# Moving a softmax sum one step later, a residual sum to GpSimd, and weight products out of the preparation, in a four-layer graph network kernel

## The chip, the core and the metric

The kernel runs on one core of one Trainium2 chip. A core has TensorE (PE in the profile; its weight loads are listed as PEld), VectorE (DVE), ScalarE (ACT), GpSimd (POOL) and SyncE (SP, here used only to issue DMA transfers), and each works through its own queue in order. The metric is the time of one execution on the device in microseconds; lower is better.

## The reference, cut to what matters

A graph has 50,000 nodes with 256 features in float32 and 25,000 edges, sorted by destination. Four layers follow each other, each with a residual and a layer norm. Layer 2 is the one with the most edits:

```python
x = _layernorm(x + L0(x, Wq, Wk, Wv, src, dst))            # attention, sum over edges, 8 heads of 32
x = _layernorm(x + L1(x, edge_index, W1, b1, W2, b2, ...)) # neighbour sum, two products, norm
x = _layernorm(x + L2(x, edge_index, W, att_src, att_dst, bias, ln_w, ln_b))
x = _layernorm(x + L3(x, edge_index, edge_attr, Wq, bq, ..., Ws, bs))

def L2(x, edge_index, W, att_src, att_dst, bias, ln_w, ln_b):   # the edges and one loop per node
    h = (x @ W).reshape(n, H, C)
    e = einsum(h, att_src)[src] + einsum(h, att_dst)[dst]
    e = where(e > 0, e, 0.2 * e)
    ex = exp(e - segment_max(e, dst)[dst])
    alpha = ex / segment_sum(ex, dst)[dst]
    out = segment_sum(h[src] * alpha, dst) + bias
    y = out + x
    return (y - mean(y)) / sqrt(var(y) + EPS) * ln_w + ln_b
```

Layer 2 therefore has two norms: its own ("inner", over the 256 features of `out + x`) with a weight and a bias, and then the common one ("outer") over `x + L2(x)`.

## The kernel before, in words

The nodes are worked on in 196 units of 256 nodes (two tiles of 128, one node to a partition). The program is a sequence of stages that follow each other: the preparation (lists of edges by node tile, weights, constants), layer 0 over edge chunks and nodes, the nodes of layer 1 together with layer 2's projection (`nodes1`, which writes the projected rows `hh_d`), the nodes of layer 2 (`nodes2`), the edges of layer 3 and the nodes of layer 3 (`nodes3`).

Within a stage nothing is scheduled by a compiler: every engine has a function `body(s, at)` that is unrolled for steps s = 0, 1, ..., and in step s a piece with lag L handles unit s - L:

```python
def run_units(total, depth, body):
    for s in range(total + depth):
        body(s, lambda lag: s - lag if 0 <= s - lag < total else None)
```

So the lag and the place in `body` set the order of an engine's queue. Engines wait for each other by semaphores, and for free places in rings of buffers. The softmax of layers 2 and 3 is made once for a group of `GU` = 8 units, with the scores laid out as one row for each node tile and head, by scans along the row: `tops` is the group whose maxima are made in this step, `shares` the one whose sums and shares (the alpha) are made.

`nodes2` in step s, before the change, engine by engine:

- SyncE loads the unit's one-hot matrix `hot` (source edge to node; a ring of `HOT` = 18), at lag 12 the projected rows `hin` and edge attributes `attr`, at lag 14 the residual input `xin` (a ring of `XR` = 9), and stores `e_row`.
- GpSimd gathers the sources' rows of the step's unit by two indirect DMAs into a ring of `NR` = 16 places, and at lag 16 adds `xin` to the node's own message `own`:

```python
if u < NR: gp.wait_ge(zeroed, u + 1)
else:      gp.wait_ge(weighed, u - NR + 1)
```

- TensorE transposes `hot` (lag 2) and `attr` (lag 14), makes the edge product with `w3_e` for layer 3 and the destination's scores, and at lag 17 aggregates: `agg = hot x weighted + bias + own`. It also turns the shares of a group (`share_ps`) at lag 14.
- VectorE, in the order of its queue: reciprocals and shifts of both norms (`norm_invert`, `norm_shift`, inner lag 19, outer lag 22), the group's scans at lag 12 (maxima) and 13 (sums), spread in between, `own` (lag 15), inner statistics on `agg` (18), outer statistics `norm_measure` (21), `scaled` = agg x ln_w (20), merging of the inner statistics (18), `weighted` = gathered rows x share (15), merging of the outer statistics (21), and last the residual sum `outer_rows` = agg + xin (L1422, lag 20).
- ScalarE copies what TensorE made (`turned`, `att_edge`, `e_row`), applies both norms (inner lag 19, outer lag 22), takes the square roots (18 and 21) and the exponential (12), and stores.

VectorE announces `weighed` after `weighted`, `inner["filled"]` comes from TensorE after `agg`, `outer["filled"]` after the residual sum, and `scaled_done` after `scaled`. Groups of layer 3 (`nodes3`) go the same way with fewer pieces.

The shift of a norm is one VectorE instruction for both tiles of a unit, `shift = moments x -1 x rstd` (L478), with two tensor operands. The preparation's VectorE work runs: masks on the edges' ends (`below_lo` and others), the first edge column of each node tile (`first_cast`, from a transfer `first_col` by SyncE), then the weight products: `w2_h` times the attention vectors, `gin`, `w3_s` plus identity, and the biases split into three bf16 parts (`b3`, `bias3`). The list of edges by tile is loaded back as `pairs` by SyncE at the head of layer 0.

## Time and profile before

| | before |
|---|---|
| median of 3 runs | 5031.09 us (5024.81 to 5033.5) |
| the profiled execution | 4998.33 us, of which the span is 4996.6 us |
| mean granted TensorE clock | 0.938 |
| busy share | PE 91%, PEld 70%, DVE 80%, ACT 56%, POOL 50% |
| DMA | 970.10 MB, mean 194 GB/s |
| stages (about, us from the start) | preparation to 55.5, layer 0 to 1093, nodes1 to 2486, nodes2 to 3600, edges of layer 3 to 4257, nodes3 to the end |

The span is the profiler's time from the first to the last instruction of the one profiled execution; the time of that execution is a little longer, and the runs beside it are without the profiler. A busy share is over the whole span, so it mixes stages with different limits; the granted clock is the share of full speed (2.4 GHz) that TensorE was given in a stretch, 0.5 being 1.2 GHz.

### The profile page before, as it was taken

To read this page: it belongs to the slowest core of one execution; us is meant where nothing else is said; L and a number is where in the kernel's file an instruction comes from. 1 tells how busy PE (TensorE), PEld (TensorE's weight loads), DVE (VectorE), ACT (ScalarE), POOL (GpSimd) and SP (SyncE) were. 2 spreads that over 40 slices of the span, in tenths; PEclk is the share of its full clock that TensorE was granted. 3 is DMA by queue.
4 is the path that set the end of the run, shared out by engine and by line. 5 is a ranking of instruction groups with operands and counts; after the bars stand their busy time and mean duration, and the time that the engine had idled before them with its cause. 6 is when DMAs were issued, how large, how long until landed. Compare 5 with 4: busy or idle time off the path is not lost. (4 is left out here: it accounts for less than half of the span.)

```text
span 4996.6 us, 90737 instructions
## 1 busy us (share of the span) xinstructions
PE 4563.9 (91%) x21673; PEld 3506.0 (70%) x21722; DVE 3986.5 (80%) x13147; ACT 2805.1 (56%) x6326; POOL 2476.3 (50%) x2462
## 2 busy tenths in 40 slices
PE   4999998779999999999888888888799999699998
PEld 3666664448888888888767777777566666577777
DVE  4777778979999999999859999999855555567666
ACT  1787886545555555555547777777611111366565
POOL 3555551237777777777466666666365554000000
PEclk8999996569999999999979999999899999899999
DMA  6777778954444444444468888787555554677775
GB/s 138 210 225 222 223 223 257 298 187 135 150 152 153 149 148 152 153 153 148 143 184 252 244 244 244 243 243 243 183 172 163 163 164 146 193 228 228 223 228 160
DMA packets 911233, 970.10 MB, mean 194 GB/s; under 512 B 104899, under 2 KB 867258, under 8 KB 910892
## 3 DMA queue, kind: packets, MB, share of 16 engines
q1 hardware_dynamic: 500692, 471.58, 32.9%
q10 hardware_dynamic: 327416, 315.35, 18.6%
q0 software_dynamic: 82784, 179.41, 12.3%
q8 instruction: 119, 1.95, 0.2%
q14 instruction: 222, 1.82, 0.1%
HBM read 654.56 MB, written 363.57 MB: 204 GB/s over the span
## 5 line engine op out<-in xcount | busy, mean ns | idle before, releaser
L1186 POOL DMA_INDIRECT nodes_near_rows<-hh_d,source_row x392 | 394.9, 1007 | 401.3 <-DVE nodes_weighted L1403 292.6
L586 POOL DMA_INDIRECT layer_xg<-in_x,edge_rows x392 | 386.7, 987 | 358.5 <-PE layer_t_ps L627 241.5
L884 POOL DMA_INDIRECT nodes_near_rows<-x_d,nodes_cur x392 | 419.0, 1069 | 238.2 <-POOL nodes_cur L879 170.8
L1542 POOL DMA_INDIRECT edges_xg<-x_d,edge_rows x392 | 372.9, 951 | 264.3 <-PE edges_x_ps L1568 172.6
L485 ACT ACTIVATE nodes_x<-nodes_outer_rows,nodes_outer_shift,nodes_outer_rstd 128x256 f32<-128x256 f32 x784 | 428.0, 597 | 61.1 <-issue 51.4
L1597 ACT ACTIVATE edges_xT<-edges_x_ps 128x512 f32<-128x512 f32 x196 | 117.1, 597 | 524.7 <-PE edges_x_ps L1568 524.7
L1806 PE MATMUL nodes_agg<-w_s,nodes_xT 128*128 128x256 f32 x1568 | 405.5, 381 | 0.0
L1004 PE MATMUL nodes_h_ps<-w_h,nodes_x2T 128*128 128x272 f32 x1568 | 392.2, 393 | 8.1 <-ACT nodes_x2T L1081 8.1
L660 PE MATMUL layer_agg<-layer_msg,layer_hot 128*128 128x264 f32 x784 | 314.2, 540 | 73.5 <-issue 65.7
L642 PE MATMUL layer_kv_ps<-w_kv,layer_xT 128*128 128x512 f32 x784 | 372.3, 597 | 1.0 <-DVE layer_made L751 1.0
L994 PE MATMUL nodes_out_ps<-w_b,nodes_hid 128*128 128x256 f32 x1568 | 371.2, 380 | 1.4 <-DVE nodes_inner_rows L925 0.8
L1014 PE MATMUL nodes_hid_ps<-nodes_zT,w_a 128*128 128x256 f32 x1568 | 370.5, 379 | 0.7 <-ACT nodes_zT L1088 0.7
L1633 DVE TENSOR_TENSOR edges_kv<-edges_kv_ps,edges_e_row 128x512 f32<-128x512 f32 x196 | 135.5, 692 | 295.2 <-PE edges_kv_ps L1584 295.2
L1584 PE MATMUL edges_kv_ps<-w_kv,edges_xT 128*128 128x512 f32 x784 | 368.4, 592 | 2.6
L660 PEld LDWEIGHTS layer_agg<-layer_msg,layer_hot 128*128 128x128 f32 x784 | 191.6, 260 | 219.3 <-issue 191.8
L1004 PEld LDWEIGHTS nodes_h_ps<-w_h,nodes_x2T 128*128 128x128 f32 x1568 | 297.3, 190 | 65.8 <-ACT nodes_x2T L1081 10.0
L899 POOL TENSOR_TENSOR nodes_x2b<-nodes_x,row_L_gnn_ln_b 128x512 f32<-128x512 f32 x196 | 265.8, 1356 | 142.0 <-DMA x_d<-nodes_x2b 131.4
L485 ACT ACTIVATE layer_y<-layer_ln_rows,layer_ln_shift,layer_ln_rstd 128x256 f32<-128x256 f32 x392 | 213.8, 592 | 217.0 <-DVE layer_ln_shift L478 217.0
L1014 PEld LDWEIGHTS nodes_hid_ps<-nodes_zT,w_a 128*128 128x128 f32 x1568 | 297.8, 190 | 46.5 <-ACT nodes_zT L1088 1.1
L1806 PEld LDWEIGHTS nodes_agg<-w_s,nodes_xT 128*128 128x128 f32 x1568 | 284.6, 191 | 31.0
L994 PEld LDWEIGHTS nodes_out_ps<-w_b,nodes_hid 128*128 128x128 f32 x1568 | 282.6, 190 | 32.4 <-issue 1.0
L941 DVE SCALAR_TENSOR_TENSOR nodes_scaled<-nodes_inner_rows,nodes_inner_moments,row_L_gnn_gamma 128x256 f32<-128x256 f32 x392 | 300.8, 806 | 0.0
(223 smaller groups left out, 12341.3 us busy)
## 6 DMA issues: line engine op xcount, KB each, us to landing
nodes_xin<-x_d SPq DMA_DIRECT2D x588, 256.0 KB, 3.8
layer_msg<-msg_d SPq DMA_DIRECT2D x392, 132.0 KB
hh_d<-nodes_hh ACTq DMA_DIRECT2D x196, 264.0 KB, 4.1
nodes_msg<-msg_d SPq DMA_DIRECT2D x392, 132.0 KB, 3.1
x_d<-layer_y ACTq DMA_DIRECT2D x196, 256.0 KB, 3.8
x_d<-nodes_x2b ACTq DMA_DIRECT2D x196, 256.0 KB, 3.5
nodes_hin<-hh_d SPq DMA_DIRECT2D x196, 256.0 KB, 3.9
x_d<-nodes_x ACTq DMA_DIRECT2D x196, 256.0 KB
```

What stands on the lines that cost most here:

```text
L485: last = nc.scalar.activation(to[:, h, :], t["rows"][:, ring(u, 4), h, :], ACT.Identity, bias=t["shift"][:, ring(u, 4), h:h + 1], scale=t[ ...
L586: gp.indirect_dma_start(out=xg[:, c % 8, k, :], out_offset=None, in_=x, in_offset=bass.IndirectOffsetOnAxis(ap=edge_rows[:, c, k:k + 1], a ...
L642: last = nc.tensor.matmul(kv_ps[b][:, :], xT[:, b, 0, i, :], w0_kv[:, i, :], start=i == 0, stop=i == KC - 1)
L660: last = nc.tensor.matmul(agg[u % 2][:, h, 0:D + H], hot[:, u % 4, h, :], msg[:, r, h, :], start=True, stop=True)
L884: gp.indirect_dma_start(out=near_rows[:, r, h, :], out_offset=None, in_=x1_d, in_offset=bass.IndirectOffsetOnAxis(ap=cur[:, r, h:h + 1], a ...
L994: last = nc.tensor.matmul(out_ps[ring(u, 2)][:, h * D:(h + 1) * D], hid[:, ring(u, 2), k, h * P:(h + 1) * P], w1_b[:, k, :], start=k == 0, ...
L1004: last = nc.tensor.matmul(h_ps[:, h, 0:D + 2 * H], x2T[:, ring(u, 2), k, h, :], w2_h[:, k, :], start=k == 0, stop=k == KC - 1)
L1014: last = nc.tensor.matmul(hid_ps[:, m * 2 * P:(m + 1) * 2 * P], w1_a[:, k, m * P:(m + 1) * P], zT[:, ring(u, 2), k, :, :].rearrange("p h n ...
L1186: gp.indirect_dma_start(out=near_rows[:, u % NR, h, :], out_offset=None, in_=hh_d, in_offset=bass.IndirectOffsetOnAxis(ap=source_row[:, 2 ...
L1542: gp.indirect_dma_start(out=xg[:, c % 8, k, :], out_offset=None, in_=x3_d, in_offset=bass.IndirectOffsetOnAxis(ap=edge_rows[:, c, k:k + 1] ...
L1584: last = nc.tensor.matmul(kv_ps[r][:, :], xT[:, b, 0, j, :], w3_kv[:, j, :], start=False, stop=j == KC - 1)
L1806: nc.tensor.matmul(to, xT[:, u % 2, k, h, :], w3_s[:, k, :], start=k == 0, stop=False)
```

## The change

There are three parts. **(1) Preparation and layer 0.** The weight products and split biases leave the preparation: they become twelve pieces that VectorE runs in twelve steps of layer 0 from step `U0` + 56, and their small loads are issued by ScalarE at the head of layer 0. Of the edges' ends only the destinations are cast before the first masks, the sources after them. The masks of layer 0 are made at `U0` + 24 instead of `U0` + 6, and the `pairs` are loaded during units 8 to 15 instead of ahead of unit 0. **(2) `nodes2`.** The sums of a group are made in step 14 instead of 13, and all that follows moves one step later: share transposes, `own` and `weighted` (15 to 16), GpSimd's own addition (16 to 17), aggregation (17 to 18), inner statistics (18 to 19), `scaled` (20 to 21), outer statistics (21 to 22), the outer shift and its application (22 to 23). `HOT` goes from 18 to 19; `NR` stays at 16. `scaled` writes to the outer norm's rows in SBUF instead of to `agg` in PSUM, and GpSimd adds `xin` to them at lag 21, as the last piece of its step; VectorE's residual sum (L1422) is gone. TensorE waits for `scaled_done` instead of `outer["filled"]` before it reuses an `agg`. The shifts are made by `norm_shift_halves`, one `tensor_scalar` for each tile. **(3) `nodes3`.** The sums and all that follows (share transpose, `weighted`, transposes of `xin`, aggregation, norm, store) are one step later; nothing else changes there.

The diff, cut to what the rest refers to (lags that only grow by one are left out):

```diff
-    LOADS = 11 + len(rows) + 2 + BV + 2
+    LOADS = 11 + len(rows) + 2
...
-                for k in (1, 0):
-                    ve.wait_ge(edges_in[k], 48)
-                    nc.vector.tensor_copy(ends_f[:, k, :, :], ends_c[:, k, :, :]).then_inc(cast, 1)
-                for k in (1, 0):
-                    last = nc.vector.tensor_copy(pairs[:, :, :, k], ends_c[:, k, :, :])
-                last.then_inc(paired, 1)
+                ve.wait_ge(edges_in[1], 48)
+                nc.vector.tensor_copy(ends_f[:, 1, :, :], ends_c[:, 1, :, :]).then_inc(cast, 1)
+                nc.vector.tensor_copy(pairs[:, :, :, 1], ends_c[:, 1, :, :])
...
+                    if mask is below_lo:
+                        ve.wait_ge(edges_in[0], 48)
+                        nc.vector.tensor_copy(ends_f[:, 0, :, :], ends_c[:, 0, :, :]).then_inc(cast, 1)
+                        nc.vector.tensor_copy(pairs[:, :, :, 0], ends_c[:, 0, :, :]).then_inc(paired, 1)
...
-                link(nc.vector.tensor_tensor(b3[:, 0:D], b3[:, 0:D], rows["L2_gnn_ln_b"][0:3, :], ALU.subtract))
...
-                link(nc.vector.tensor_copy(bias3[0:3, :], b3_sum[:, :]))
...
+    def norm_shift_halves(ve, t, u):
+        ve.wait_ge(t["inverted"], num(u) + 1)
+        for h in range(2):
+            last = nc.vector.tensor_scalar(t["shift"][:, ring(u, 4), h:h + 1], t["moments"][:, ring(u, 4), h, 0:1],
+                                           t["rstd"][:, ring(u, 4), h:h + 1], -1.0, ALU.mult, ALU.mult)
+        last.then_inc(t["shifted"], 1)
...
-        MASKS = U0 + 6
+        MASKS, WEIGHTS = U0 + 24, U0 + 56
...
-                sp.wait_ge(lists_out, 16)
-                for h in range(H):
-                    sp.dma_start(pairs[h * 2 * GU:(h + 1) * 2 * GU, 0:WHOLE, :],
-                                 windows[0:WHOLE * 2 * GU, :].rearrange("(g w) x -> w g x", w=2 * GU)).then_inc(pairs_in, 16)
-                    sp.dma_start(pairs[h * REST:(h + 1) * REST, WHOLE, :], windows[WHOLE * 2 * GU:TILES, :]).then_inc(pairs_in, 16)
                 for u in range(UNITS):
+                    if 8 <= u < 8 + H:
+                        h = u - 8
+                        sp.wait_ge(lists_out, 16)
+                        sp.dma_start(pairs[h * 2 * GU:(h + 1) * 2 * GU, 0:WHOLE, :],
+                                     windows[0:WHOLE * 2 * GU, :].rearrange("(g w) x -> w g x", w=2 * GU)).then_inc(pairs_in, 16)
+                        sp.dma_start(pairs[h * REST:(h + 1) * REST, WHOLE, :], windows[WHOLE * 2 * GU:TILES, :]).then_inc(pairs_in, 16)
...
+                for k, name in enumerate(("L2_gnn_att_src", "L2_gnn_att_dst")):
+                    act.dma_start(att[:, k, :], row(a[name], D)).then_inc(more_in, 16)
+                for k, name in enumerate(split_biases):
+                    act.dma_start(b3[:, k * D:(k + 1) * D], row(a[name], D, 3)).then_inc(more_in, 16)
...
+                def weights(piece):
+                    if piece == 0:
+                        ve.wait_ge(more_in, (2 + BV) * 16)
+                        link(nc.vector.tensor_tensor(b3[:, 0:D], b3[:, 0:D], rows["L2_gnn_ln_b"][0:3, :], ALU.subtract))
+                        nc.vector.tensor_scalar(gin[:, :], gin[:, :], 1.0, None, ALU.add)
+                    elif piece <= 2 * KC:
+                        k, j = (piece - 1) // 2, (piece - 1) % 2
+                        link(nc.vector.tensor_tensor(wprod[:, :], w2_h[:, k, 0:D], att[:, j, :], ALU.mult))
+                        link(nc.vector.tensor_reduce(watt[:, k, j * H:(j + 1) * H],
+                                                     wprod[:, :].rearrange("p (h c) -> p h c", h=H), axis=AX.X, op=ALU.add))
+                    elif piece == 2 * KC + 1:
+                        nc.vector.tensor_copy(w2_h[:, :, D:D + 2 * H], watt[:, :, :])
+                    elif piece <= 3 * KC + 1:
+                        k = piece - 2 * KC - 2
+                        nc.vector.tensor_tensor(w3_s[:, k, k * P:(k + 1) * P], w3_s[:, k, k * P:(k + 1) * P], ident[:, :], ALU.add)
+                    elif piece <= 3 * KC + 4:
+                        k = piece - 3 * KC - 2
+                        link(nc.vector.tensor_copy(b3_part[:, :], b3[:, :]))
+                        link(nc.vector.tensor_tensor(b3[:, :], b3[:, :], b3_part[:, :], ALU.subtract))
+                        if k == 0:
+                            link(nc.vector.tensor_scalar(b3_sum[:, :], b3_part[:, :], ident[0:3, 0:1], None, ALU.mult))
+                        else:
+                            link(nc.vector.scalar_tensor_tensor(b3_sum[:, :], b3_part[:, :], ident[0:3, k:k + 1], b3_sum[:, :],
+                                                                ALU.mult, ALU.add))
+                    else:
+                        link(nc.vector.tensor_copy(bias3[0:3, :], b3_sum[:, :]))
...
+                    if WEIGHTS <= s < WEIGHTS + 12:
+                        weights(s - WEIGHTS)
...
-        NR, HR, XR, WR, HOT, LATER = 16, 5, 9, 4, 18, 12
+        NR, HR, XR, WR, HOT, LATER = 16, 5, 9, 4, 19, 12
...
-                    u = at(16)
+                    u = at(17)
                     if u is not None:
                         gp.wait_ge(own_done, u + 1)
                         gp.wait_ge(x_in[u % XR], u // XR * 16 + 16)
                         gp.tensor_tensor(own[:, u % WR, :, :], own[:, u % WR, :, :], xin[:, u % XR, :, :], ALU.add).then_inc(based, 1)
-                run_units(UNITS, 16, body)
+                    u = at(21)
+                    if u is not None:
+                        scaled = outer["rows"][:, u % 4, :, :]
+                        gp.wait_ge(scaled_done, u + 1)
+                        gp.tensor_tensor(scaled, scaled, xin[:, u % XR, :, :], ALU.add).then_inc(outer["filled"], 1)
+                run_units(UNITS, 21, body)
...
-                            pe.wait_ge(outer["filled"], u - 3)
+                            pe.wait_ge(scaled_done, u - 3)
...
-                    tops, shares = (g // GU if g is not None and g % GU == 0 else None for g in (at(12), at(13)))
-                    u = at(19)
+                    tops, shares = (g // GU if g is not None and g % GU == 0 else None for g in (at(12), at(14)))
...
-                        norm_shift(ve, inner, (None, 8, u))
-                    u = at(22)
-                    if u is not None:
-                        norm_shift(ve, outer, (None, 8, u))
+                    u = at(20)
+                    if u is not None:
+                        norm_shift_halves(ve, inner, (None, 8, u))
+                    u = at(23)
+                    if u is not None:
+                        norm_shift_halves(ve, outer, (None, 8, u))
...
-                        nc.vector.tensor_tensor(in_halves(agg[u % 4]), in_halves(agg[u % 4]), both(rows["L2_gnn_ln_w"]), ALU.mult)\
+                        if u >= 4:
+                            ve.wait_ge(outer["normed"], u - 3)
+                        nc.vector.tensor_tensor(outer["rows"][:, u % 4, :, :], in_halves(agg[u % 4]), both(rows["L2_gnn_ln_w"]), ALU.mult)\
...
                             .then_inc(scaled_done, 1)
...
-                    u = at(15)
+                    u = at(16)
                     if u is not None:
                         of_tiles = head_columns(share_ps, of_group(u // GU))
                         ve.wait_ge(share_turned, u // GU + 1)
...
-                    u = at(20)
-                    if u is not None:
-                        ve.wait_ge(scaled_done, u + 1)
-                        ve.wait_ge(x_in[u % XR], u // XR * 16 + 16)
-                        if u >= 4:
-                            ve.wait_ge(outer["normed"], u - 3)
-                        nc.vector.tensor_tensor(outer["rows"][:, u % 4, :, :], in_halves(agg[u % 4]), xin[:, u % XR, :, :], ALU.add)\
-                            .then_inc(outer["filled"], 1)
```

## Rows read from the trace of the kernel before

**Rows 1.** Windows: stretch, length, busy PE, PEld, DVE, ACT, POOL (xinstructions), clock, DMA share, GB/s:

```profile
55.50:125.00 69.50, 46.49 (x155) 29.54 (x156) 22.29 (x57) 13.81 (x36) 42.67 (x45) 0.77 0.86 182
125.00:790.00 665.00, 662.82 (x2583) 409.34 (x2581) 478.74 (x1885) 526.41 (x1005) 347.90 (x352) 1.00 0.72 217
2623.50:3488.40 864.90, 763.73 (x4362) 641.35 (x4360) 793.41 (x2800) 622.76 (x1561) 526.35 (x480) 0.93 0.80 245
```

**Rows 2.** Timeline, GpSimd, 3019 to 3028: start, duration, instruction, idle before it:

```profile
3019.22 1.02 POOL L1186 DMA_INDIRECT nodes_near_rows<-hh_d,source_row  x1 [4.13 <-DVE nodes_weighted L1403]
...
3021.57 1.27 POOL L1193 TENSOR_TENSOR nodes_own<-nodes_own,nodes_xin 128x512 f32<-128x512 f32 x1
3023.55 1.02 POOL L1186 DMA_INDIRECT nodes_near_rows<-hh_d,source_row  x1 [0.72 <-issue]
```

**Rows 3.** Timeline, VectorE and TensorE, one ordinary step:

```profile
3020.71 0.73 DVE L458 BATCH_NORM_STATS2 nodes_outer_parts<-nodes_outer_rows 128x6 f32<-128x256 f32 x2
...
3022.11 0.65 DVE L1403 TENSOR_TENSOR nodes_weighted<-nodes_near_rows,nodes_share_ps 128x512 f32<-128x512 f32 x1
...
3022.84 0.66 DVE L1422 TENSOR_TENSOR nodes_outer_rows<-nodes_agg,nodes_xin 128x512 f32<-128x512 f32 x1
...
3023.26 0.44 PE L1250 MATMUL nodes_work_ps<-ident,nodes_hot 128*128 128x128 f32 x2
...
3027.65 0.20 PEld L1250 LDWEIGHTS nodes_work_ps<-ident,nodes_hot 128*128 128x128 f32 x2 [0.21 <-ACT nodes_e_row L1489]
```

**Rows 4.** Waits, 2500 to 3600: who waits, for whom: total us, times, longest:

```profile
POOL nodes_near_rows L1186 <- DVE nodes_weighted L1403: 292.6, 145, 4.1
DVE nodes_outer_rstd L474 <- ACT nodes_outer_dev L469: 53.1, 54, 2.3
DVE nodes_score_ps L1133 <- ACT nodes_score_ps L1499: 30.5, 25, 3.2
```

**Rows 5.** Window in a group's softmax:

```profile
3005.00:3011.00 6.00, 5.09 (x15) 3.64 (x16) 6.00 (x26) 3.73 (x10) 3.29 (x3) 0.50 0.40 127
```

**Rows 6.** Timeline, VectorE and GpSimd, the step with the sums:

```profile
3002.69 0.72 DVE L458 BATCH_NORM_STATS2 nodes_outer_parts<-nodes_outer_rows 128x6 f32<-128x256 f32 x2
...
3005.09 0.65 DVE L1403 TENSOR_TENSOR nodes_weighted<-nodes_near_rows,nodes_share_ps 128x512 f32<-128x512 f32 x1
...
3006.53 1.02 POOL L1186 DMA_INDIRECT nodes_near_rows<-hh_d,source_row  x1 [3.54 <-DVE nodes_weighted L1403]
```

**Rows 7.** Groups: count | busy us, mean ns of one | idle before:

```profile
L899 POOL TENSOR_TENSOR nodes_x2b<-nodes_x,row_L_gnn_ln_b 128x512 f32<-128x512 f32 x196 | 265.8, 1356 | 142.0 <-DMA x_d<-nodes_x2b 131.4
...
L478 DVE SCALAR_TENSOR_TENSOR nodes_inner_shift<-nodes_inner_moments,nodes_inner_rstd 128x2 f32<-128x2 f32 x195 | 49.8, 255 | 0.1
...
L478 DVE SCALAR_TENSOR_TENSOR nodes_outer_shift<-nodes_outer_moments,nodes_outer_rstd 128x2 f32<-128x2 f32 x192 | 29.9, 156 | 0.0
```

**Rows 8.** Timeline, a held shift and GpSimd's addition:

```profile
3013.48 1.63 DVE L478 SCALAR_TENSOR_TENSOR nodes_inner_shift<-nodes_inner_moments,nodes_inner_rstd 128x2 f32<-128x2 f32 x1
...
3013.81 1.27 POOL L1193 TENSOR_TENSOR nodes_own<-nodes_own,nodes_xin 128x512 f32<-128x512 f32 x1
```

**Rows 9.** Timeline of the preparation and the head of layer 0:

```profile
15.75 0.29 DVE L344 CAST prepare_ends_f<-prepare_ends_c 98x256 f32<-98x256 int32 x1 [7.22 <-DMA prepare_ends_c<-in_src]
...
39.93 0.40 DVE L375 TENSOR_TENSOR prepare_b<-prepare_b,row_L_gnn_ln_b 3x256 f32<-3x256 f32 x1
...
41.58 0.32 SPq L304 DMA_DIRECT2D first_col<-first_edges  x1
...
53.85 0.68 DVE L393 CAST bias<-prepare_b_sum 3x1024 bf16<-3x1024 f32 x1
...
121.36 2.10 PE L660 MATMUL layer_agg<-layer_msg,layer_hot 128*128 128x264 f32 x4 [7.88 <-DMA layer_msg<-msg_d]
```

**Rows 10.** DMA issues: name, engine, count, KB each:

```profile
layer_pairs<-windows SPq DMA_DIRECT2D x8, 384.0 KB
```

**Rows 11.** Timeline, TensorE, layer 3's nodes:

```profile
4514.49 0.30 PE L1785 MATMUL nodes_share_ps<-ident,nodes_share 128*128 128x128 f32 x1 [1.87 <-DVE nodes_weighted L1718]
```

More of the change, by code:

```diff
@@ L218, in marked, with row @@
         return mark, settle
+    def row(ap, n, parts=P):
+        return bass.AP(ap.tensor, ap.offset, [[0, parts], [1, n]])
     def prepare(sb, ps, sem, sems, block):
@@ L253, in prepare @@
         first_cast, first_out, first_in, d, pl = sem("first_cast"), sem("first_out"), sem("first_in"), sem("d"), sem("pl")
-        def row(ap, n, parts=P):
-            return bass.AP(ap.tensor, ap.offset, [[0, parts], [1, n]])
         with block() as blk:
@@ L272, in _ @@
                     load(t[:, :], row(a[name], D))
-                for k, name in enumerate(("L2_gnn_att_src", "L2_gnn_att_dst")):
-                    load(att[:, k, :], row(a[name], D))
-                for k, name in enumerate(split_biases):
-                    load(b3[:, k * D:(k + 1) * D], row(a[name], D, 3))
                 load(gin[:, :], row(a["L1_gnn_eps"], 1))
@@ L1700, in body @@
                     group = group_at(at)
-                    u = at(20)
+                    u = at(21)
                     if u is not None:
                         norm_invert(ve, ln, (None, 8, u))
-                    u = at(15)
+                    u = at(16)
                     if u is not None:
@@ L1724, in body @@
                         mark(top_run(g, n, run[0:n, :], score_ps[0:n, 0:P]))
-                    g = group(12)
+                    g = group(13)
                     if g is not None:
@@ L1729, in body @@
                         mark(sum_run(g, n, run[0:n, :], grown[0:n, :]))
-                    g = group(13)
+                    g = group(14)
                     if g is not None:
@@ L1734, in body @@
                         mark(nc.vector.reciprocal(total[0:n, :], total[0:n, :]))
-                    g = group(14)
+                    g = group(15)
                     if g is not None:
@@ L1757, in body @@
                         nc.vector.tensor_tensor(less[0:n, :], score_ps[0:n, 0:P], top[0:n, :], ALU.subtract).then_inc(less_ready, 1)
-                    g = group(12)
+                    g = group(13)
                     if g is not None:
@@ L1778, in body @@
                         nc.tensor.transpose(score_ps[0:n, 0:P], score[:, 0:n], ident[:, :]).then_inc(score_turned, 1)
-                    g = group(15)
+                    g = group(16)
                     if g is not None:
```

104 lines of the change are left out of this document (44 added, 60 removed).

## The prediction

> **What bounds the kernel now.** I read the stage windows first, then the waits of layer 2's nodes, then its timeline engine by engine, then the two ends of the change (the preparation and the layer 3 nodes). The stages run one after another, so each has its own limit. The long stages that the change touches are layer 0 (TensorE without a gap from 125 us to 790 us), layer 2's nodes and layer 3's nodes. In layer 2's nodes a unit takes 5.41 us: in the steady window of 864.9 us GpSimd has 480 instructions, three to a unit, so 160 units [rows 1]. An ordinary step takes less: GpSimd starts its first gather at 3019.22 and again at 3023.55, 4.33 us later [rows 2]. In such a step three engines are nearly tied. VectorE has no idle time. TensorE goes from transposes to transposes in 4.39 us (3023.26 to 3027.65), and its last wait there is for ScalarE's `e_row` [rows 3]. GpSimd spends 0.7 us before its first gather, 2.35 with the two gathers and 1.28 in the own-message addition, which is all of 4.33 [rows 2]. The missing 1.08 us per unit is lost once per group of eight, around the softmax: the scan waits for ScalarE's exponential (30.5 us in all), VectorE for the outer root (53.1 us) [rows 4], and after TensorE's idle time there its granted clock is 0.50, the 1.2 GHz level, from 3005 to 3011 us [rows 5]. The row that decides this case is another: GpSimd waits 145 times, 292.6 us, for VectorE's `weighted` before it may gather [rows 4]. Its ring of sources has NR = 16 places, `weighted` of unit v is made in step v + 15, and so the gather of step s waits for step s - 1 of VectorE. When the product ends late (3005.09 + 0.65), the gather starts 0.79 us after that end, at 3006.53 [rows 6].
>
> **The change in layer 2's nodes.** It moves `weighted` to step v + 16 and leaves NR at 16. The gather of GpSimd's step s now waits for unit s - 16, which VectorE makes in its own step s, late in it. Behind the gathers, in GpSimd's one queue, stand the own-message addition (unit s - 17) and, new, the residual sum of unit s - 21. VectorE's step s + 1 opens its outer statistics with exactly that sum (`norm_measure(outer)` at lag 22), and makes `weighted` behind them. This closes a ring through two engines, once per step. Each piece has a row:
> - end of `weighted` to the start of the first gather: 0.79 [rows 6];
> - first gather to the start of the own addition: 3021.57 - 3019.22 = 2.35 [rows 2];
> - own addition: 1.28 (1.27 in the row shown) [rows 2]; the residual sum is the same operation on the same shape in SBUF, so 1.28 again. No row shows it in that place; the lower bound is VectorE's 0.66 for the sum that it replaces, the upper one 1.36 (GpSimd's layer 1 sum with a broadcast row) [rows 3, 7];
> - semaphore to VectorE: about 0.05; then start of the outer statistics to the end of `weighted`: 3022.11 + 0.65 - 3020.71 = 2.05 [rows 3].
>
> The sum is 0.79 + 2.35 + 1.28 + 1.28 + 0.05 + 2.05 = 7.80 us a step against 5.41 a unit. Only VectorE work between the outer statistics and `weighted` adds to it. In the step with the sums that is 3005.74 - 3002.69 - 2.05 = 1.0 us [rows 6]; in the step with the maxima I take 0.5 (the less and the top operation, two instructions of the smaller kind). So 1.5 per group. What VectorE saves (0.66 less the price of two more shift instructions at 0.08 spacing each), what it no longer waits for at the scan, and the shifts that are no longer long all lie in the 5.7 us in which it waits for GpSimd, and are worth nothing.
>
> The ring holds from step 21, when the first residual sum is due, to step 195, the last gather: 175 steps with 22 groups. 175 x (7.80 - 5.41) + 22 x 1.5 = 418 + 33 = 451 us. Before step 21 and in the drain I take -5 in all: there GpSimd has no gather in front of the sum, and VectorE has one operation less.
>
> TensorE is then idle for some 3 us in each step, more than the idle time that already costs its clock in every group, so part of its steps will run at 1.2 GHz. Of an ordinary step's 4.39 us about 0.5 is ScalarE's two copies at the end; at half the clock the step is 2 x 3.9 + 0.5 = 8.3 [rows 3, 5]. It may start its aggregation when the own sum is there, 4.4 us after `weighted`, and VectorE needs its result some 12 us after that, so it just fits; in the step with the shares and in that with the scores it is up to 2.5 us late. 0 to 55 us over 22 groups; I take 15, since the clock rises again while it is busy.
>
> A rule of the Trainium skill bears on the sum: GPSIMD Engine Reference, section "Elementwise — side-by-side cycle accounting", has a two-input GpSimd operation at about 2.6 cycles an element, which for 512 elements at 1.2 GHz is an estimate of 1.1 us, and the same page advises against elementwise work there. By that the ring would be 0.2 us shorter and the whole 31 us less; the trace has 1.28, so the row is taken.
>
> **The shift per tile.** `nodes_inner_shift` takes 0.16 us as a rule, but 1.63 us at 3013.48, when GpSimd's own addition (3013.81 + 1.27 = 3015.08) ends just before it does [rows 8]. The groups agree over the stage: 49.8 us for the inner shift, 29.9 for the outer, as many instructions [rows 7]. The new form has one tensor operand instead of two and should not be held. Worth 20 us at most, were VectorE the bound; here nothing. The Trainium skill, SBUF — State Buffer, section "SBUF: two separate sides", says that a VectorE operation with two SBUF inputs and a GpSimd operation that reads SBUF exclude each other; the 1.63 agrees.
>
> **The preparation.** VectorE's weight products run from 39.93 to 54.53 us and end the stage [rows 9]. What is left after `first_cast` is SyncE's round trip: the column of first edges is issued at 41.58 and lands some microseconds later; I take 44.5, so 10 us go. The masks also no longer wait for the sources at 15.75 [rows 9]: the destination's chain starts 6.9 us sooner, of which I take 6. Together -16 (bounds -10 and -18). Layer 0 then opens without the 3 MB of pairs (8 x 384 KB) [rows 10] in front of its x and message loads; TensorE waited 7.88 us for the first message [rows 9], and its clock is 0.77 there [rows 1]. I take -12 (0 to -20). The pairs now travel in units 8 to 15 under a DMA share of 0.72 [rows 1], at no cost as long as TensorE has its chunks; if that cover goes, 3 MB at 217 GB/s are 14 us. The 14.6 us of weight products lie in twelve steps of layer 0 where VectorE is busy 478.74 of 665 us; free time in 12 steps of 7 us is 24 us, but pieces of 3 us are not smooth: +3 (0 to 14.6). ScalarE issues six small loads before its table load, while the first gather is under way: +2 (0 to 6). Together -23.
>
> **Layer 3's nodes.** TensorE loses 1.87 us a group at the share transpose, waiting for `weighted` [rows 11]. Sum, reciprocal, share and transpose all move by one step together, so the same product is late in the same way: VectorE passes three short steps instead of two after the table load and has one scan more in them. I cost it at nothing (within 0.6 us a group, 15 us either way) plus 2 us for one more unit of filling.
>
> **Sum.** 451 - 5 + 15 - 23 + 2 = 440. The profiled execution took 4998.33 us (span 4996.6); it lies 33 us under the median of the runs. 4998 + 440 + 33 = 5471, say 5470 us.
>
> **Rivals.**
> 1. *The ring also hangs on TensorE at 1.2 GHz.* For it: every idle stretch of this length in a group drops the clock. Against: it is released while busy. If every step takes 8.3 us instead of 7.8: +88 and up to 2.5 us a group more, about 5600 us at most. Chance 0.11.
> 2. *No ring, only throughput.* GpSimd's own step, 0.79 + 2.35 + 1.28 + 1.28 = 5.70, would be the period if the outer sum were needed later than I think: 175 x 0.29 = 51, less 23: 5060 us. Against: the lags 21 and 22 and the order in the queue. Chance 0.06.
> 3. *Faster.* If a gather's place in the ring were free a step before it is asked for, GpSimd would make the residual sum before VectorE wants it, and VectorE's relief would count: the scan's wait (30.5) and the held shifts (20) go, ordinary steps stay at TensorE's and ScalarE's 4.4. 4998 - 50 - 23 + 33 = 4958. It decides from 17 places or more; the 292.6 us of waiting at 16 with an earlier product speak against. Chance 0.07.
> 4. *The gains at the start and the costs cancel*, within 10 us of 5031: only with the ring open and GpSimd's 5.70 half hidden. Chance 0.02.
>
> The forecast has 0.74; its own range, from a ring of 7.6 to 8.0 us and the terms above, is 5420 to 5560. With rival 1 the range is 5400 to 5600 and leaves out less than 2 in 10. A measurement of this kernel tells about 0.2% (10 us) from no change: faster 0.07, same 0.02, slower 0.91.
>
> **What would show it.** In the profile after: the span of layer 2's nodes some 460 us longer; first gathers 7.8 us apart; GpSimd's wait for `nodes_weighted` still there, now in nearly every step, and a wait of some 3 us of VectorE's outer statistics for GpSimd's new sum; GpSimd about 5 us busy in 8; TensorE's clock well under 0.93; VectorE's share down. Preparation over near 39 us. Wrong if gathers start before the product of the same step, or if the outer statistics don't wait.

## The result and the profile after

The changed kernel takes 5474.81 us (5474.42 to 5475.28) and the kernel before, on the same chip, 5030.78 us: a ratio of 1.0884 (1.0866 to 1.0903), 444 us slower. The profiled execution after has a span of 5473.6 us, 477 more than that of before.

The waits of layer 2's nodes after, 2500 to 4200 us (engine, line, for whom: us in total, times, longest), which answer to [rows 4]:

```profile
POOL nodes_near_rows L1208 <- DVE nodes_weighted L1432: 557.6, 178, 8.7
...
PE nodes_agg L1292 <- issue: 348.2, 164, 5.0
DVE nodes_outer_parts L430 <- POOL nodes_outer_rows L1220: 288.3, 158, 4.5
```

The gather's wait for the product is there in 178 steps, and it has a counterpart that the kernel before didn't have: VectorE's outer statistics wait 158 times for GpSimd's residual sum. Two engines that wait for each other in every step are the sign of a ring in the prediction's sense: a loop of waits in which each piece needs the one before it, and the last needs the first of the step before (not to be confused with a ring of buffers). Its pieces can be read one behind the other in the timeline of one step after:

```profile
3309.74 1.02 POOL L1208 DMA_INDIRECT nodes_near_rows<-hh_d,source_row  x1 [2.90 <-DVE nodes_weighted L1432]
...
3312.07 1.28 POOL L1215 TENSOR_TENSOR nodes_own<-nodes_own,nodes_xin 128x512 f32<-128x512 f32 x1
3313.29 1.27 POOL L1220 TENSOR_TENSOR nodes_outer_rows<-nodes_outer_rows,nodes_xin 128x512 f32<-128x512 f32 x1
...
3314.60 0.75 DVE L430 BATCH_NORM_STATS2 nodes_outer_parts<-nodes_outer_rows 128x6 f32<-128x256 f32 x2 [2.84 <-POOL nodes_outer_rows L1220]
...
3316.01 0.65 DVE L1432 TENSOR_TENSOR nodes_weighted<-nodes_near_rows,nodes_share_ps 128x512 f32<-128x512 f32 x1
...
3317.46 1.01 POOL L1208 DMA_INDIRECT nodes_near_rows<-hh_d,source_row  x1 [2.90 <-DVE nodes_weighted L1432]
```

From gather to gather it is 3317.46 - 3309.74 = 7.72 us: 2.33 to the own addition, 2.49 for both additions, 0.04 to the statistics, 2.06 to the end of the product, 0.80 to the next gather. Over all steps from 21 to 195 the first gathers stand 7.99 us apart (5.40 before, counted in the same way), 7.74 to 7.82 in six steps of a group, 8.30 in the one with the maxima and 8.88 in the one with the sums.

Windows after: start and head of layer 0, its steady part, the ring (columns as in [rows 1]):

```profile
41.00:110.50 69.50, 43.63 (x160) 27.73 (x161) 22.28 (x57) 14.17 (x37) 43.58 (x46) 0.77 0.49 146
110.50:775.50 665.00, 657.13 (x2564) 405.14 (x2563) 487.99 (x1888) 521.18 (x996) 347.75 (x351) 1.00 0.75 220
2700.00:3450.00 750.00, 543.97 (x2554) 431.34 (x2553) 435.91 (x1736) 366.03 (x917) 423.56 (x376) 0.83 0.55 166
```

In the third row no engine is busy for even three quarters of the time: this is what a stage looks like that is bound by latency round a ring. TensorE's granted clock has fallen from 0.93 [rows 1] to 0.83, and yet TensorE isn't what the ring waits for. The DMA share at the head of layer 0 is 0.49 instead of 0.86, since the `pairs` come later; the clock there is 0.77 as before.

The groups of the instructions that the change touches, in layer 2's nodes after (count | busy us, mean ns | idle before), which answer to [rows 7]:

```profile
L1215 POOL TENSOR_TENSOR nodes_own<-nodes_own,nodes_xin 128x512 f32<-128x512 f32 x196 | 249.3, 1272 | 4.6
L1220 POOL TENSOR_TENSOR nodes_outer_rows<-nodes_outer_rows,nodes_xin 128x512 f32<-128x512 f32 x196 | 248.8, 1269 | 48.7 <-DVE nodes_outer_rows L1410 48.7
...
L456 DVE TENSOR_SCALAR nodes_outer_shift<-nodes_outer_moments,nodes_outer_rstd 128x1 f32<-128x1 f32 x392 | 63.7, 204 | 0.1
L456 DVE TENSOR_SCALAR nodes_inner_shift<-nodes_inner_moments,nodes_inner_rstd 128x1 f32<-128x1 f32 x392 | 61.7, 199 | 0.1
```

The new addition costs what the old one does, 1.27 us. The shift in halves is no longer held (199 and 204 ns), but as two instructions it takes 125 us of VectorE's time in all where the single one took 80 [rows 7]. None of the 784 is longer than 0.22 us, where 14 of the 392 before took 1.3 to 1.7 us, one of them the 1.63 of [rows 8]. The Trainium skill, SBUF — State Buffer, section "SBUF: two separate sides", has a VectorE operation take the lock on the shared ports only when it has two SBUF inputs (and then only against a GpSimd operation that reads SBUF) or runs in a two-port mode; both traces agree.

Where the difference lies, by stage (each from its first instruction to that of the next, read from the timelines), in the profile of before and after, and in that of a repaired kernel (the first experiment below):

| us | before | after | after, gathers later |
|---|---|---|---|
| preparation | 55.5 | 41.0 | 39.1 |
| layer 0 | 1023.0 | 1029.5 | 1013.4 |
| nodes of layer 1 | 1413.7 | 1415.2 | 1415.8 |
| nodes of layer 2 | 1120.5 | 1595.5 | 1114.9 |
| of these: gather 0 to gather 21 | 74.0 | 95.8 | 78.7 |
| of these: gather 21 to gather 195 | 939.9 | 1389.8 | 930.7 |
| edges of layer 3 | 647.3 | 662.5 | 648.9 |
| nodes of layer 3 | 736.7 | 729.8 | 728.2 |

### The profile page after: what moved, and what is told of

It reads as the page before. It is cut to its first block and busy times, and to the rows that moved or that the text cites. A ratio compares the mean times of both kernels' runs of the same rounds, so it can differ in the third digit from the quotient of the medians.

```text
span 5473.6 us, 91131 instructions
## 1 busy us (share of the span) xinstructions
PE 4740.2 (87%) x21673; PEld 3604.6 (66%) x21722; DVE 3930.2 (72%) x13343; ACT 2800.5 (51%) x6324; POOL 2711.2 (50%) x2658
## 5 line engine op out<-in xcount | busy, mean ns | idle before, releaser
L1292 PE MATMUL nodes_agg<-nodes_weighted,nodes_hot 128*128 128x256 f32 x784 | 333.5, 517 | 353.2 <-issue 348.2
L430 DVE BATCH_NORM_STATS2 nodes_outer_parts<-nodes_outer_rows 128x6 f32<-128x256 f32 x784 | 291.0, 413 | 288.6 <-POOL nodes_outer_rows L1220 288.3
L1292 PEld LDWEIGHTS nodes_agg<-nodes_weighted,nodes_hot 128*128 128x128 f32 x784 | 176.0, 248 | 412.5 <-issue 389.5
```

Of the source, the lines that this page charges most:

```text
L1292: nc.tensor.matmul(cols, hot[:, u % HOT, h, :], weighted[:, u % WR, h, :], start=True, stop=False)
```

## The experiments

The kernel before took 4998 us on the chip of the first four runs, 4997 us on that of the next four, and 5026 us on that of the last four; each ratio is against the kernel before on the same chip. The profiled execution of before that the prediction reads (4998.33 us) agrees with the first two chips, its timed runs with the third. So times are compared within a group of four, and across the groups only ratios and the stretch from gather 21 to gather 195 of layer 2's nodes ("us a unit" below), which the profiles repeat well: 1389.8 and 1388.5 us for the changed kernel at its two times, 939.9 to 940.0 for the three kernels with the old code there.

### 1. The gathers one step later

```diff
 # nodes2, GpSimd, in the changed kernel
-                    u = at(0)
+                    u = at(1)
                     if u is not None:
                         if u < NR:
```

> The changed kernel with GpSimd's gathers one step later (unit s - 1 in step s), nothing else: the same work on every engine, but a gather now waits for the product that VectorE made a step before, so the ring of gather, residual sum, outer statistics and product is closed over two steps, 4.0 us each, and no longer sets the pace. Ring theory: GpSimd's own step (2.35 + 1.27 + 1.27 + about 0.3 = 5.2 us) or the softmax steps set it, 5.2 to 5.8 us a unit in layer 2's nodes, in all 5000 to 5100 us. Rival (more work for GpSimd, or GpSimd and VectorE hold each other up, whatever the order): nearly the 7.99 us a unit of the changed kernel stay, over 5350 us.

4964.6 us, ratio 0.9935 (0.9919 to 0.9952). A lag of one more takes back the whole loss and gains 33 us on the kernel before of its chip. The result lies 35 us below the range of the ring theory, which had been reckoned from 5475 us on a slower chip, and nearly 400 us below the rival's. GpSimd's queue in its timeline:

```profile
3301.99 1.01 POOL L1208 DMA_INDIRECT nodes_near_rows<-hh_d,source_row  x1 [0.16 <-issue]
3303.31 1.00 POOL L1208 DMA_INDIRECT nodes_near_rows<-hh_d,source_row  x1 [0.30 <-issue]
3304.33 1.28 POOL L1215 TENSOR_TENSOR nodes_own<-nodes_own,nodes_xin 128x512 f32<-128x512 f32 x1
3305.55 1.28 POOL L1220 TENSOR_TENSOR nodes_outer_rows<-nodes_outer_rows,nodes_xin 128x512 f32<-128x512 f32 x1
3306.99 1.02 POOL L1208 DMA_INDIRECT nodes_near_rows<-hh_d,source_row  x1 [0.16 <-issue]
```

and the window of its steady part:

```profile
2700.00:3450.00 750.00, 654.96 (x3808) 557.66 (x3808) 639.04 (x2583) 542.30 (x1363) 632.45 (x561) 0.95 0.82 247
```

The gather waits 0.16 us, for nothing but its own issue; GpSimd is full in an ordinary step, 5.00 us. A rival by which GpSimd simply has too much work is out: it does the same work here in 632 of 750 us. A step without a long wait takes 5.0 to 5.3 us against 4.3 to 4.5 before (one of 4.9), but of the three long steps of a group (6.46, 7.16 and 7.11 us before) one is left, 7.06. In all it is 5.35 us a unit against 5.40. The new addition isn't what takes the gain back: with the sum on VectorE (experiments 5 and 12) an ordinary step is 4.7 us and the unit 5.35 us again. What holds the group at 42.8 us was not isolated. The gain over the kernel before is in the table's other stages: the later sums and the moved residual sum give 6 us in layer 2's nodes, the other two parts the rest (experiments 7 and 8).

### 2. The own addition ahead of the gathers

```diff
 # nodes2, GpSimd's body, in the changed kernel
+                    u = at(17)    # own addition, moved up
+...
                     u = at(0)     # gathers
 ...
-                    u = at(17)
-...
                     u = at(21)    # residual sum
```

> The changed kernel with GpSimd's own-message addition moved ahead of the gathers in its step. The ring stays but is shorter by exactly that one instruction, 1.27 us. Ring theory: first gathers 7.99 - 1.27 = 6.72 us apart, 175 steps x 1.27 = 222 us less, so about 5250 us (5230 to 5275). Rival (GpSimd has too much work): the same work in another order, no change from 5475 us.

5209.7 us, ratio 1.0422 (1.0405 to 1.0439). First gathers are 6.74 us apart (6.72 expected), so the ring is a sum of its pieces: take one instruction of 1.27 us out of it and each step is 1.25 us shorter. The time in us was missed, 5250 expected, because it was reckoned from 5475 on a chip where the kernel before takes 33 us more; from this chip's 4998 the ratio is what the ring gives.

### 3. Both additions ahead of the gathers

The same with the residual sum moved up as well.

> The changed kernel with both of GpSimd's additions ahead of the gathers. The residual sum no longer stands behind the gather that waits for the product, so there is no ring. Ring theory: a step is 5.3 to 5.8 us (gathers behind a residual sum that waits for the scaled rows of the same step), 5010 to 5120 us. Rival (too much work for GpSimd, or engines that hold each other up): over 5350 us.

4963.82 us, ratio 0.9931 (0.9915 to 0.9948), 5.36 us a unit; the expected range, 5010 to 5120, was reckoned from the slower chip again and missed by 46 us. The order of three pieces in one queue, with every wait and every ring of buffers as in the changed kernel, is enough to open the ring.

### 4. The residual sum back on VectorE

```diff
 # nodes2, in the changed kernel: GpSimd
-                    u = at(21)
-                    if u is not None:
-                        scaled = outer["rows"][:, u % 4, :, :]
-                        gp.wait_ge(scaled_done, u + 1)
-                        gp.tensor_tensor(scaled, scaled, xin[:, u % XR, :, :], ALU.add).then_inc(outer["filled"], 1)
 # TensorE: waits for outer["filled"] again; VectorE: scaled in agg again, and as its last piece
+                    u = at(21)
...
+                        nc.vector.tensor_tensor(outer["rows"][:, u % 4, :, :], in_halves(agg[u % 4]), xin[:, u % XR, :, :], ALU.add)\
+                            .then_inc(outer["filled"], 1)
```

> The changed kernel with the residual sum back on VectorE, one step later than in the kernel before; the gathers wait for the product of the same step as in the changed kernel. Ring theory: without the residual sum behind the gathers there is no ring, although the wait is as tight as in the changed kernel; the start of the stage stays some 20 us longer than before, the steady steps are those of the kernel before or a little shorter since the sums have a step more: 4960 to 5060 us. Rival (the later product alone, with NR at 16, makes the gathers late and costs the time): over 5300 us.

5391.11 us, ratio 1.0787 (1.0769 to 1.0805). This was 331 us above the expected range, and the rival's range came true: the later product alone, with 16 places, costs nearly as much. A second ring stands right behind the first. Its trace, from one gather to the one two steps on:

```profile
3303.61 1.02 POOL L1208 DMA_INDIRECT nodes_near_rows<-hh_d,source_row  x1 [8.14 <-DVE nodes_weighted L1425]
...
3305.96 1.27 POOL L1215 TENSOR_TENSOR nodes_own<-nodes_own,nodes_xin 128x512 f32<-128x512 f32 x1
...
3307.34 1.19 PE L1287 MATMUL nodes_agg<-nodes_weighted,nodes_hot 128*128 128x256 f32 x2 [3.70 <-POOL nodes_own L1215]
...
3311.30 1.67 PE L1296 MATMUL nodes_work_ps<-w_e,nodes_turned 128*128 128x256 f32 x4
...
3313.45 0.38 ACT L1511 ACTIVATE nodes_e_row<-nodes_work_ps 128x256 f32<-128x256 f32 x1
...
3313.72 0.30 ACT L441 ACTIVATE nodes_outer_dev<-nodes_outer_moments,eps_ln 128x2 f32<-128x2 f32 x1
...
3314.04 0.17 DVE L446 RECIPROCAL nodes_outer_rstd<-nodes_outer_dev 128x2 f32<-128x2 f32 x1 [5.18 <-ACT nodes_outer_dev L441]
...
3317.55 0.65 DVE L1425 TENSOR_TENSOR nodes_weighted<-nodes_near_rows,nodes_share_ps 128x512 f32<-128x512 f32 x1
...
3319.00 1.02 POOL L1208 DMA_INDIRECT nodes_near_rows<-hh_d,source_row  x1 [6.53 <-DVE nodes_weighted L1425]
```

Gathers, own addition, TensorE's aggregation (which wants the own sum), behind it in TensorE's queue the edge product, behind that in ScalarE's queue the copies and the outer root, then VectorE's outer reciprocal at the head of its step, the product, and the gather: 3319.00 - 3303.61 = 15.39 us for two steps, 7.70 a step; the mean over the stage is 7.74. In this step TensorE comes back from 3.70 us of idling at a low clock:

```profile
3307.00:3313.50 6.50, 6.17 (x20) 4.66 (x20) 1.86 (x8) 0.44 (x3) 3.52 (x4) 0.57 0.24 57
```

A granted clock of 0.57, near the 1.2 GHz level: aggregation and edge product take 5.6 us (3307.34 to 3312.97) where the same chain takes 2.98 at the full clock later in that trace. Over the stage it is the same in every second unit: TensorE idles 2.9 to 3.7 us before the aggregation, the granted clock of the chain is 0.53 to 0.64 and it takes 4.8 to 5.6 us (means by the unit's place in its group); in the units between there is no idle time, the clock is 1.0 and the chain takes 2.98. So the ring makes TensorE idle, the clock is low after the idle time, and the low clock lengthens the ring.

### 5. The residual sum on VectorE, the own addition ahead of the gathers

The kernel of 4 with the edit of 2.

> The run with the residual sum back on VectorE took 5391 us, which the first ring alone can't explain. Its trace shows a second ring over two steps: gathers of step s, own addition behind them, TensorE's aggregation in step s + 1, ScalarE's copies and outer root behind it, VectorE's outer reciprocal at the head of step s + 2, product, gathers; 15.4 us in all. This kernel takes the own addition ahead of the gathers, which cuts that ring and leaves the product as late and NR at 16. Second-ring theory: back to the pace of the kernel before, 5.2 to 5.5 us a unit in layer 2's nodes, and with the gains outside them 4930 to 5010 us beside some 4998 us of before on such a chip. Rival (the late product makes the gathers late and these the scores, whatever stands behind them): over 5300 us as without the swap.

4967.68 us, ratio 0.9943 (0.9928 to 0.9958), inside the range of the second-ring theory. Out of the gathers' shadow, the own addition closes no ring; 5.35 us a unit. GpSimd still waits for the product in 176 steps:

```profile
POOL nodes_near_rows L1213 <- DVE nodes_weighted L1425: 314.0, 176, 8.7
```

As long a wait as before's [rows 4], in as many steps as after's, and it costs nothing: what decides is what stands behind the waiting instruction and who wants it.

### 6. The kernel before with the own addition first

> The kernel before with GpSimd's own addition ahead of the gathers, nothing else. In the kernel before the second ring spans three steps, so 15.4 us at TensorE's lower clock and some 12.5 us at the higher one leave 5.1 or 4.2 us a step against 5.41 measured. Theory A: that ring has slack on the mean but binds in the softmax steps, where the clock is low; cutting it gains 10 to 60 us. Theory B: it never binds, within 0.2% of before.

4989.01 us, ratio 0.9984 (0.9975 to 0.9993), 5.34 us a unit instead of 5.40; gather 21 to gather 195 takes 928.6 us instead of 939.9, and the last long step of a group goes from 7.11 to 6.33 us. By the medians it is 8 us less: clear of no change, but just under the 10 to 60 us of theory A. The two traces don't bear out its mechanism either. In the kernel before, TensorE's aggregation starts within 0.4 us of the end of the own addition in 1 of 196 units, and waits 0.3 us for it in all (in experiment 4, 91 units and 293 us): the second ring over three steps doesn't bind there. What goes away is the held inner shift of [rows 8]:

```profile
L478 DVE SCALAR_TENSOR_TENSOR nodes_inner_shift<-nodes_inner_moments,nodes_inner_rstd 128x2 f32<-128x2 f32 x196 | 30.6, 156 | 0.1
```

That is 156 ns on the mean instead of 255 [rows 7]. In the kernel before the 14 shifts of over 1 us all lie in that last long step, which takes 7.76 us in the 14 groups that have one and 5.85 in the other 8. With the own addition ahead of the gathers none is longer than 0.52 us, and the step is 6.85 and 5.74 us by turns. So the held shifts cost the kernel before some 0.9 us in 14 groups, which is about what this experiment gains. That they alone do it is read from the traces and was not tested; the kernel before with the shift in halves would be the test.

### 7 and 8. The other two parts alone

The kernel before with the change's first part, and with the change of layer 3's nodes, each by itself.

> The kernel before with the first part of the change alone (casts, weight products and split biases moved, masks and pairs later). By the prediction's terms -23 us (-16 preparation, -12 head of layer 0, +3 and +2). The stage table of the runs so far shows -16 for the preparation and -10 for layer 0, so -26: a ratio of 0.995. Rival (layer 0 pays the moved work back): within 0.2% of before.

4970.0 us, ratio 0.9944 (0.9931 to 0.9958), 27 us less by the medians. Layer 0 doesn't pay the moved work back.

> The kernel before with the later sums in layer 3's nodes alone. By the prediction's term +2 us. The stage table of the runs so far shows 8 us less in that stage, so rather -8 us, a ratio of 0.998: TensorE waits less for the product ahead of the share transposes. If it is +2, the 8 us belong to the stages ahead of it.

4991.15 us, ratio 0.9986 (0.9977 to 0.9995), 6 us less by the medians. Its wait at the share transposes, to be read beside [rows 11]:

```profile
PE nodes_share_ps L1785 <- DVE nodes_weighted L1718: 38.9, 24, 1.6
```

In the kernel before this wait is 45.0 us in 24 groups, so the 6 us are here.

### 9. The changed kernel again, on a third chip

> The changed kernel once more, unchanged, on the chip of the experiments, where the kernel before takes 4997 us and not 5031. Its first profile has some 15 us more than the profile of before or of any experiment in each of three places where nothing was changed to account for it: the head of layer 0, the first steps of layer 2's nodes (gather 16 starts 65.8 us after gather 0, 50.5 in the other kernels with the later lags) and the edges of layer 3. If these belong to that chip, this run takes 5474.8 - 33 = 5442 us or less, down to 5430, and the three places are as in the others. If they belong to the kernel, 5470 us. The steady steps are 7.99 us in either case.

5468.44 us, ratio 1.0874 (1.0858 to 1.0891). The chip of this group was not as I had written, it takes 5026 us for the kernel before. So the time alone decides nothing; but the same three places are long again. One of them shows in the single wait of VectorE for the first `fifth` of layer 2 (the scores times 0.2, which ScalarE makes). In the changed kernel's first profile:

```profile
DVE nodes_score_ps L1354 <- ACT nodes_fifth L1473: 38.5, 1, 38.5
```

and in the kernel of experiment 1:

```profile
DVE nodes_score_ps L1354 <- ACT nodes_fifth L1473: 23.3, 1, 23.3
```

All four kernels profiled on this chip have layer 0 at 1030 to 1031 us and the edges of layer 3 at 662 to 663 us, and 90 to 97 us from gather 0 to gather 21 of layer 2's nodes; all eight on the other two chips have 1013 to 1022, 647 to 649 and 74 to 80. So these some 45 us come with the chip (or with whatever else sets that group of runs apart) and not with the changed kernel. The kernel before loses only some 30 there (5026 or 5031 against 4997), so up to 15 may belong to the changed start or lags on such a chip; there is no profile of the kernel before from one, and both this and what such a chip does differently stay open.

### 10 to 12. Both repairs together, the old shift, the sum on VectorE with later gathers

Experiment 10 has the edits of 1 and 3 together, experiment 12 those of 4 and 1.

> The changed kernel with both repairs, gathers a step later and both additions ahead of them. With either alone a unit takes 5.35 us in layer 2's nodes. If what is left there is still GpSimd's queue, the two together are faster than each, down to 5.2 us a unit, 4935 us; if it is the softmax step of 7.06 us and TensorE (655 of 750 us busy), no change: 4960 to 4968 us. I expect the second.

5013.65 us, ratio 0.9972 (0.9962 to 0.9982), 5.36 us a unit: as expected no gain over one repair.

```diff
 # nodes2, VectorE, in the kernel of experiment 1
-                        norm_shift_halves(ve, inner, (None, 8, u))
+                        norm_shift(ve, inner, (None, 8, u))
...
-                        norm_shift_halves(ve, outer, (None, 8, u))
+                        norm_shift(ve, outer, (None, 8, u))
```

> The changed kernel with gathers a step later and the norm shifts as one instruction with two tensor operands again. The held shifts cost up to 20 us of VectorE's time in the kernel before; VectorE is busy 639 of 750 us here, so it has slack and I expect no difference from 4964.6 us, 4958 to 4972. If the port that GpSimd holds matters, more GpSimd additions now hold it more often: up to 4985 us.

5016.31 us, ratio 0.9979 (0.997 to 0.9988).

> The changed kernel with the residual sum back on VectorE and gathers a step later: what the move of the residual sum to GpSimd is worth with no ring closed. With the sum on VectorE and the own addition first a unit took 5.35 us, the same as with the sum on GpSimd and no ring, so I expect 4960 to 4972 us, and the move is worth nothing. If VectorE's 0.66 us a unit counts, 4980 us or more. If GpSimd's 1.27 us counts, 4950 us or less.

5015.07 us, ratio 0.9975 (0.9965 to 0.9986), 5.35 us a unit.

The medians agree within 3 us on one chip. The kernel of experiment 1 was not run on that chip, so the finer reading goes by gather 21 to gather 195 in the profiles. There the engine of the residual sum moves nothing once no ring is closed: 931.6 us with the sum on VectorE, 930.7 with it on GpSimd. The old shift costs a little: 935.8 us. It is held far more often than in the kernel before, since GpSimd has twice the additions; 92 shifts take 0.27 to 1.75 us, and together they cost VectorE 58 us more than at 0.16 each, of which the stage pays 5:

```profile
L450 DVE SCALAR_TENSOR_TENSOR nodes_inner_shift<-nodes_inner_moments,nodes_inner_rstd 128x2 f32<-128x2 f32 x196 | 86.8, 443 | 0.1
```

All three missed their us (4935 to 4985 expected) because the chip is slower by some 30 to 50. Against the kernel before they gain 10 to 13 us here, where experiments 1 and 3 gained 33 and 34 on a chip of the other kind; these 20 to 24 us are the open difference of experiment 9 again, and somewhat more than the 15 put down to it there.

## Why the prediction was right, point by point

- **The ring** is where it was put and of the size that was worked out. The pieces, as means over steps 24 to 191 of the profile after: end of product to gather 0.80 (0.79 predicted), gather to own addition 2.38 (2.35), additions 1.27 + 1.27 (1.28 each), residual sum to the end of the next product 2.32 (0.05 + 2.05 + 1.5/8 = 2.29), less 0.05 that the records of two additions overlap. In all 7.99 (7.80 + 0.19), and 450 us from gather 21 to 195 (451). Experiments 1, 2 and 3 each open or shorten it as its sum says.
- **What it missed: the second ring.** The prediction lists the steps' lags for the first ring only and holds, in rival 2, that without the residual sum in the ring there would be 5060 us. Experiment 4 has the residual sum elsewhere and 5391 us on a chip where before takes 4998. The first ring hides the second by 0.25 us a step. So the forecast was right because the longer ring was the one that I had seen; "the residual sum on GpSimd costs 444 us" would be a wrong reading. The cause that is shown is the product a step later against 16 places and the additions behind the gathers: take away either, and the whole loss is gone (experiments 1, 3 and 5). Experiment 1 gives the gather the same lead over its place as a 17th place would; more places themselves were not tried.
- **TensorE's clock, +15.** It fell (0.83), but next to nothing of it is on the first ring: the step with the maxima is 0.5 us longer and that with the sums 1.0 by their VectorE pieces, as was reckoned, and VectorE's outer statistics start late by another 0.15 and 0.08 us in two steps of a group. This term was 5 us at most. In the second ring, where TensorE stands in the chain, the clock does count.
- **Start and drain of the stage, -5.** On the chips of the faster kind a kernel with the later lags takes 79 us to gather 21 against 74, so +5, and the drain (from the last gather on) of the profile after is 3.4 longer: +8. A later product also fills the pipeline later; that was forgotten.
- **The start, -23.** -27 (-21 to -34) measured alone: preparation -14.5 to -18.8 in the kernels that have this part, the rest in layer 0.
- **Layer 3's nodes, +2.** -6 (-2 to -11). The step that failed is "the same product is late in the same way": TensorE's wait at the share transposes is 0.25 us shorter in each of the 24 groups.
- **The shift per tile, nothing.** Nothing in the changed kernel, where the shift is no piece of the ring. Elsewhere it is worth something: 5 us without a ring (experiment 11), and by the traces of experiment 6 some 11 us in the kernel before.
- **The 33 us between the profile and the median.** They were added, and the sum met the median to 5 us. In part that is luck: with the terms as measured on a chip of the faster kind, 450 + 5 + 8 - 27 - 6 = 430 take the place of 440, and the open difference of experiment 9 makes up the rest to 444. The 33 us are a difference between chips: the profile after, from the slower kind, lies on its median, and the difference of the two spans is 477 and not 440. Of the 37 us more, 27 are in the stage's start, 15 in the edges of layer 3 and 14 in layer 0 (the three places of experiment 9), less 15 for the clock; the other terms nearly cancel.
- **Rival 3** said 4958 us with a place freed one step earlier, 73 us below its chip's 5031. Experiment 1 is that case, and it gained 33, most of it in the stages outside layer 2's nodes. Of the 50 us that the rival gave to layer 2's nodes 6 came. An ordinary step doesn't stay at 4.4 us, since GpSimd's two gathers and two additions fill 5.00; but with the sum on VectorE it is no better over a group (experiment 12), so the rival's price fails by more than that.

## What to carry to other kernels

When an instruction is moved by one step in a software pipeline, write down every ring that passes through a buffer's reuse: the wait for the free place, what stands behind the waiting instruction in its queue, who needs that, and how many steps later the loop is back; the price of a step is the sum of the pieces over the number of steps. Do it for all followers in the queue and not only for the one that is new, and look for the ring next in length before you say what a fix would bring. Such a loss is cheap to mend: a wait taken one step later, or short pieces put ahead of the instruction that waits, costs no memory and gave back everything here. Before a gain from such a swap is put down to a ring, look whether the waits of that ring are in the trace: in experiment 6 they aren't, and a held instruction is what went away.

## What was not expected of the hardware

Chips differ by stage and not evenly: with the same code for the stage it was 12 to 18 us more in the head of layer 0, in the first steps of layer 2's nodes and in the edges of layer 3, in the four profiles from one chip and in the changed kernel's first one, and within 2 us the same time everywhere else (1415 to 1416 us in layer 1's nodes, 728 to 730 in layer 3's changed nodes, 7.98 and 7.99 us a step in the ring). A profile and a median taken on different chips can't be set against each other to 0.5%.

And a loop of waits through TensorE lengthens itself: with TensorE idle in every second step of experiment 4 the granted clock was 0.57 in the busy stretch shown, and its share of the loop 5.6 us instead of 2.98.

The price of a held VectorE instruction depends on where it falls. In the kernel before 14 holds of 1.3 to 1.7 us, all in the last long step of a group, go with about 0.9 us each; in experiment 11, 92 holds with 58 us in all cost 5.
